# Attention on one Trainium2 core: the Wo projection and its add to x inside the attention loop

## What is computed

```
x = x + 0.5 * ffn0(layernorm(x))
x = x + attn0(layernorm(x), Wq, Wk, Wv, Wo, lam)
x = x + 0.5 * ffn0(layernorm(x))
x = x + 0.5 * ffn1(layernorm(x))
x = x + attn1(layernorm(x), ...)              # a gated delta rule
x = x + 0.5 * ffn1(layernorm(x))

attn0: q, k, v = x @ Wq, x @ Wk, x @ Wv; q, k = rope(q), rope(k)
  a1 = softmax(q[:64] @ k[:64] / 8), a2 = softmax(q[64:] @ k[64:] / 8)   # each row sees the last 64 keys
  diff = relu(a1 - lam[h] * a2); diff = diff / (sum(diff) + 1e-6)
  return concat_heads(diff @ v) @ Wo           # (1024, 2048) @ (2048, 256)
```

## Time and profile before

| | |
|---|---|
| three runs | 1872.32 us median (1869.02 to 1873.83) |
| profiled execution | 1875.38 us, its span 1873.4 us |
| PE, matmuls | 1599.8 us busy (85% of the span) |
| PE, weight loads | 1067.9 us (57%) |
| DVE | 1332.4 us (71%) |
| ACT | 1071.6 us (57%) |
| POOL | 41.2 us (2%) |
| attention loop | about 141 to 406.5 us from the span's start |
| projection with Wo, and add | 406.6 to 468.1 us |

### The profile page before, as it was taken

One profiled execution on the slowest core, in us unless ns is written; L12 is line 12 of the kernel. 1 busy time (PEld: TensorE's weight loads), 2 busy tenths in 40 slices (PEclk: granted clock), 3 DMA queues, 4 the chain that ended last, 5 costly groups with the idle time before them and its releaser, 6 DMA issues. The chain is left out here.

```text
span 1873.4 us, 32717 instructions
## 1 busy us (share of the span) xinstructions
PE 1599.8 (85%) x10728; PEld 1067.9 (57%) x10728; DVE 1332.4 (71%) x3702; ACT 1071.6 (57%) x2752; POOL 41.2 (2%) x49
## 2 busy tenths in 40 slices
PE   7867777689879857999999999999998999988678
PEld 3534434354344424676677767766766777677434
DVE  6648999830761347888988899889889888984121
ACT  6217888850621164577668766766676686653210
POOL 0000000000000000000000000000000000000000
PEclk9887998859899877999999999999999999989589
DMA  2022001000110020110211011011101110110010
GB/s 99 24 73 41 13 10 49 1 1 0 74 53 21 17 81 13 38 54 11 56 55 53 11 58 52 18 52 52 57 11 56 55 54 11 47 29 7 1 50 23
DMA packets 83989, 69.39 MB, mean 37 GB/s; under 512 B 58592, under 2 KB 72544, under 8 KB 82544
## 3 DMA queue, kind: packets, MB, share of 16 engines
q1 hardware_dynamic: 83824, 67.30, 12.0%
HBM read 58.32 MB, written 6.98 MB: 35 GB/s over the span
## 5 line engine op out<-in xcount | busy, mean ns | idle before, releaser
L1488 DVE SCALAR_TENSOR_TENSOR arena<-arena 128x1024 f32<-128x1024 f32 x144 | 184.2, 1279 | 33.6 <-ACT arena L1075 32.8
L762 PE MATMUL bank<-xt,arena 128*128 128x512 f32 x384 | 199.6, 654 | 4.5 <-ACT arena L1067 3.1
L602 PE MATMUL bank<-xt,arena 128*128 128x512 f32 (+2 forms) x384 | 178.8, 623 | 20.3 <-DMA arena<-f_ds 13.8
L1546 DVE COPY_PREDICATED arena<-arena,bank 128x512 f32<-128x512 int32 x160 | 185.6, 1179 | 0.0
L815 PE MATMUL bank<-arena 128*64 128x64 f32 x3072 | 144.1, 238 | 35.9 <-DVE arena L1568 21.9
L815 PEld LDWEIGHTS bank<-arena 128*64 128x64 f32 x3072 | 117.3, 144 | 84.0 <-issue 55.3
L1566 DVE TENSOR_TENSOR arena<-arena 128x512 f32<-128x512 f32 x224 | 157.0, 701 | 4.1 <-PE bank L815 3.7
L602 PEld LDWEIGHTS bank<-xt,arena 128*128 128x128 f32 (+2 forms) x384 | 70.9, 189 | 121.6 <-issue 99.2
L1008 ACT ACTIVATE arena<-arena 128x128 f32<-128x128 f32 x256 | 99.6, 390 | 33.5 <-DVE arena L1421 33.5
L762 PEld LDWEIGHTS bank<-xt,arena 128*128 128x128 f32 x384 | 74.3, 211 | 76.0 <-issue 73.0
L621 PE MATMUL bank<-arena 128*128 128x256 f32 (+2 forms) x384 | 101.7, 413 | 10.4 <-DVE arena L1313 9.6
(11 more groups left out here) (171 smaller groups left out, 3555.3 us busy)
## 6 DMA issues: line engine op xcount, KB each, us to landing
arena<-zero_scratch SPq DMA_DIRECT2D x29, 512.0 KB, 4.2
arena<-d_w SPq DMA_DIRECT2D x16, 519.0 KB, 6.5
arena<-beta_scratch SPq DMA_DIRECT2D x16, 512.0 KB, 5.5
arena<-f_up SPq DMA_DIRECT2D x2, 1408.0 KB, 6.7
arena<-w_scratch SPq DMA_DIRECT2D x2, 1376.0 KB, 6.1
arena<-f_idx SPq DMA_DIRECT2D x2, 1072.0 KB, 10.1
w_scratch<-arena SPq DMA_DIRECT2D x2, 1072.0 KB, 4.1
arena<-a_wq SPq DMA_DIRECT2D x16, 128.0 KB, 2.3
```

The source lines that it names most:

```text
L602: last = pe.matmul(bank[2 * w + n % 2][0:rows, :], (WU if f < 2 else WU1R)[:, w, k, m * P:m * P + rows], XT[:, k, hf * HALF:(hf + 1) * HAL ...
L762: last = pe.matmul(bank[b][:], DW[:, par, c:c + P], XT[:, k, rhs], start=(k == 0), stop=(k == KC - 1))
L1488: dve.scalar_tensor_tensor(out=CT[:, x], in0=RAW[:, x, 3 - j:3 - j + S], scalar=DW[:, par, tap:tap + 1], in1=CT[:, x], op0=ALU.mult, op1=A ...
L1546: dve.copy_predicated(out, mask, bank[b][:].rearrange("p (c b s) -> p c b s", c=8, s=s)).then_inc(free[b], 1)
```

## The change

The projection moves into the loop. For each group g and tile t, two halves of two heads each (`weighted`, 4 matmuls of 256 columns for both halves) have OT as the stationary operand and Wo as the moving one, so the result comes out untransposed in bank 5, two tiles beside each other. `out_parts` gives four slots to a pair of tiles: both halves of the first tile, a half of the second, the other half, nothing. So group 0 is projected in iterations 16 to 31, group 1 in 32 to 47, group 2 in 48 to 62, and group 3 in 63 to 70, one whole tile in each. DVE adds two tiles at a time to x in the iteration after their last half, ahead of `diff2`: 16 adds instead of 4. `weigh` shares bank 4 with `turn` now. Everything after `mask` comes one iteration later, and ACT's order is changed. Wo is loaded before the 12 loads of Wq. The transposes, YTR and its copies go.

```diff
+def out_parts(p):
+    if p < PAIRS - 1:
+        g, at = divmod(p - 2 * NT, 2 * NT)
+        j, step = divmod(at, 4)
+        return [(g, 2 * j + t, half) for t, half in (((0, 0), (0, 1)), ((1, 0),), ((1, 1),), ())[step]] if g >= 0 else []
+    return [(G - 1, p - PAIRS + 1, half) for half in range(2)] if p < PAIRS - 1 + NT else []
+
+def out_sums(p):
+    return [(g, t // 2) for g, t, half in out_parts(p - 1) if t % 2 and half]
...
+                sp.dma_start(WO, a_wo).then_inc(wo_loaded, 16)
                 for h in range(4, H):
                     sp.wait_ge(rp_done, ROPE_DONE["q", h - 4])
                     sp.dma_start(WQ[:, h % 4], a_wq[h]).then_inc(at_wq[h % 4], 16)
-                sp.dma_start(WO, a_wo).then_inc(wo_loaded, 16)
...
                     wait(pe, pt_copied, p)
+                    wait(pe, ot_copied, p - 1)
...
-                    o = bank[5][:, 0:2 * P].rearrange("p (i q) -> p i q", i=2)
+                    o = bank[4][:, 2 * P:4 * P].rearrange("p (i q) -> p i q", i=2)
...
+                def weighted(g, t, half):
+                    if half == 0:
+                        pe.wait_ge(wo_loaded, 16)
+                        pe.wait_ge(ot_copied, 16 * g + NT + t + 1)
+                        wait(pe, wo_added, 4 * g + t // 2)
+                    for h in range(2 * half, 2 * half + 2):
+                        last = pe.matmul(bank[5][:, t % 2 * D:(t % 2 + 1) * D], OT[:, 4 * g + h, t * P:(t + 1) * P],
+                                         WO[:, 4 * g + h, :], start=(h == 0), stop=(h == 3))
+                    if t % 2 and half:
+                        last.then_inc(wo_done, 1)
...
-                for p in range(PAIRS + 4):
-                    staggered(p, [(0, scores), (3, turn), (4, weigh)])
+                for p in range(PAIRS + NT):
+                    staggered(p, [(0, scores), (4, turn), (5, weigh)])
                     for m in rope_starts(p):
                         rope_project(m)
+                    for g, t, half in out_parts(p):
+                        weighted(g, t, half)
-            def project_out(a, u, ots):
...
-                project_out(0, 1, (ot_copied, PAIRS))
...
-                    wait(act, pv_done, p - 1)
+                    wait(act, pv_done, p)
...
-                             bank[5][:, 0:2 * P].rearrange("p (i q) -> p i q", i=2)).then_inc(ot_copied, 1)
-                for p in range(PAIRS + 5):
-                    staggered(p, [(3, pt_copy), (0, lambda p: exps(p, 0)), (2, norm), (0, lambda p: exps(p, 1)), (1, relu),
-                                  (4, ot_copy)])
-            def wo_copy(a):
...
+                             bank[4][:, 2 * P:4 * P].rearrange("p (i q) -> p i q", i=2)).then_inc(ot_copied, 1)
+                for p in range(PAIRS + 6):
+                    staggered(p, [(1, lambda p: exps(p, 0)), (4, pt_copy), (5, ot_copy), (3, norm), (1, lambda p: exps(p, 1)),
+                                  (2, relu)])
...
+                def add_out(g, j):
+                    dve.wait_ge(wo_done, 4 * g + j + 1)
+                    wait(dve, wo_added, 4 * (g - 1) + j + 1)
+                    x = X[:, 2 * j:2 * j + 2, :]
+                    last = dve.tensor_tensor(x, bank[5][:].rearrange("p (t d) -> p t d", t=2), x, ALU.add)
+                    last.then_inc(wo_added, 1)
+                    if g == G - 1:
+                        dve.wait_ge(wo_added, 4 * g + j + 1)
+                        dve.memset(TICK[:, 4 + j:5 + j], 0.0).then_inc(x_ready, 1)
...
-                for p in range(PAIRS + 2):
+                for p in range(PAIRS + NT + 1):
                     parts = rope_parts(p)
-                    staggered(p, [(2, norm1), (0, lambda p: mask(p, 0)), (2, norm2), (0, lambda p: mask(p, 1)), (1, diff1)])
+                    staggered(p, [(3, norm1), (0, lambda p: mask(p, 0)), (3, norm2), (0, lambda p: mask(p, 1)), (2, diff1)])
                     for m, part in parts[:len(parts) // 2]:
                         rope(m, part)
-                    staggered(p, [(1, diff2), (1, diff3)])
+                    for g, j in out_sums(p):
+                        add_out(g, j)
+                    staggered(p, [(2, diff2), (2, diff3)])
```

More of the change, by code:

```diff
@@ L280, in macaron @@
         A = Arena(arena, H * D)
-        YTR = arena[:, A.at:A.at + 2 * KC * HALF].rearrange("p (b n s) -> p b n s", b=2, n=KC)
         KZ = A.take(G, WIN + S)
@@ L380, in macaron @@
         ot_copied = sem("ot_copied")
-        wo_loaded, wo_done, wo_copied, wo_turned = sem("wo_loaded"), sem("wo_done"), sem("wo_copied"), sem("wo_turned")
+        wo_loaded, wo_done, wo_added = sem("wo_loaded"), sem("wo_done"), sem("wo_added")
         dr_const, dr_set = sem("dr_const"), sem("dr_set")
@@ L1036, in ot_copy @@
                     act.copy(OT[:, 2 * k:2 * k + 2, t * P:(t + 1) * P],
-                             bank[5][:, 0:2 * P].rearrange("p (i q) -> p i q", i=2)).then_inc(ot_copied, 1)
-                for p in range(PAIRS + 5):
-                    staggered(p, [(3, pt_copy), (0, lambda p: exps(p, 0)), (2, norm), (0, lambda p: exps(p, 1)), (1, relu),
-                                  (4, ot_copy)])
-            def wo_copy(a):
-                for n in range(4):
-                    act.wait_ge(wo_done, 4 * a + n + 1)
-                    act.copy(YTR[:, n // 2, n % 2, :], bank[n % 2][:]).then_inc(wo_copied, 1)
+                             bank[4][:, 2 * P:4 * P].rearrange("p (i q) -> p i q", i=2)).then_inc(ot_copied, 1)
+                for p in range(PAIRS + 6):
+                    staggered(p, [(1, lambda p: exps(p, 0)), (4, pt_copy), (5, ot_copy), (3, norm), (1, lambda p: exps(p, 1)),
+                                  (2, relu)])
             def dr_prelude():
@@ L1222, in _ @@
                 attention()
-                wo_copy(0)
             if count > 2:
@@ L1685, in _ @@
                 attention()
-                add_out(0, 1)
             if count > 2:
```

## The result

The changed kernel takes 1824.24 us (median of 4 runs, 1821.74 to 1829.46) against 1871.88 (4 runs): ratio 0.9744, 95% interval 0.972 to 0.9768, so 47.6 us or 2.6% faster. The prediction was 1831, range 1820 to 1854. The profiled execution has a span of 1823.5 us against 1873.4. One of the five executions of a later experiment, e3_old_lags, took 5042 us where the others took 1832 to 1842; the ratio leaves it out, the median counts it.

What follows compares the result with a forecast made beforehand. DVE was taken to bound the loop with rope, ACT without it, then PE alone for 61.6 us; -61.6 + 6.9 - 2.4 + 2 + 12.1 + 2 = -41.0 us from 1872.3 gave 1831, range 1820 to 1854.

Steps and rivals of the forecast that it cites:

- What is removed, and the tail: Behind the loop: the 61.6 us of PE alone go; the new PE-paced tail adds 12.1, plus 2 for half clock.
- The +2 for a stretch at half clock: In the tail: a stretch or two of PE's work at half clock adds 2 us.
- The adds on DVE: Iterations 19 to 55: ten adds of 0.69 us where DVE bounds, +6.9 us; two later ones hidden.
- Late scores: DVE's waits before the mask: six, 4.8 us, come at PE's half clock; half of that is gained, -2.4.
- Late PE: Iterations with rope: PE's added matmuls delay the next scores and pt_copy, +2 us, bounds 0 and 5.5.
- the worst iteration: Every eighth iteration: PE has two halves and a projection, 5.3 us; five such, 1.1 us over each.
- 0 for it, and 0.1 x 8 at most later: ACT's 15.8 us of waits for the mask go, but gain 0 where ACT is not the bound, little later.
- Costs put at nothing for ACT: ACT's queue: pt_copy's new wait for weigh of the pair before, holding back ot_copy, norm and exps, costs 0.
- the 12 that were named as a sign of being wrong: Sign against the forecast: ACT's pt_copy waiting for PE more than 12 us in all.
- A half at 0.244 us per record: PE's added matmuls: 256-column records at 0.244 us, a half of 4 records 0.98 us, all 62.5.
- the cold tail: Rival: PE at half clock from iteration 56 through the tail, +21.6 us, 1853 us; chance 0.12.
- PE as the bound: Rival: PE's waits for ACT stay, iterations take 4.55 us, not 4.2, 1847 us in all; chance 0.16.

Runs made afterwards that it cites:

- e3_old_lags: The changed kernel with the lags of before (turn 3, weigh 4, exps 0, norm 2, relu 1), ACT's changed order kept: 1838.4 us, 0.9805 of the kernel before.
- e8: The changed kernel with the free slot first, group 3 from iteration 64 and in banks 6, 7, 5, 6: 1824.1 us, 0.9744 of the kernel before.
- e4: The changed kernel without the 12 adds to x of the first three groups, a small memset in their place: 1809.0 us, 0.9662 of the kernel before.
- e2: The changed kernel's lags, ACT order, shared bank 4 and early Wo load, but the old dense projection behind the loop: 1861.0 us, 0.9927 of the kernel before.
- e10: The changed kernel with the free slot first and group 3 in banks 6, 7, 5, 6 from iteration 63: 1808.7 us, 0.9657 of the kernel before.

## Why the prediction was right

The direction held, and so did the main mechanism: the stretch with PE alone is gone, and the loop takes the projection for little. That the time within the loop came out as forecast is luck in part: errors of opposite sign, as large as what they left.

- **What is removed, and the tail**: -61.6 + 12.1 + 2 = -47.5 predicted; from the mask of pair 63 to the layer norm 72.3 became 24.8, -47.5. Two errors cancel in this match. The step had no wait on bank 5: PE waited 5.1 us for adds there, and e8 shows that without it the stretch is 5.8 shorter. And PE's work behind the mask, 23.1 us, was sized 4.1 too long, since e8 takes 19.0 at full clock: PE's iteration 63 begins 3.0 us before that mask (388.57 against 391.59), and a tile takes 1.82 us, not 1.96. The +2 for a stretch at half clock was real: eight records took 3.56 us instead of 1.89.
- **The adds on DVE**: +6.9 predicted, about 9.0 measured (e4). The mis-sized term is what the add delays, not the add: in iterations 31 and 47 it stood ahead of a rope sum for which PE's scores wait.
- **Late scores, -2.4 with ends at 0 and -4.8**: mis-sized, and split in two. The six waits away from a new group are all gone; their iterations take 23.0 us and took 28.9. The step gave more work on PE, and the clock with it, as the reason. The clock is full in these iterations now, but the waits are gone in e2 as well, without that work. But at a new group the scores became later: all masks together waited 9.5 us from 200 to 420 us, where they had waited 7.6.
- **Late PE, +2**: 2.0 by e4 against e2, and up to 2.4 more where iteration 16 is long. I had named the worst iteration and spread it over five places; it fell on two or three.
- **"0 for it, and 0.1 x 8 at most later", the stage**: the step that failed. Light iterations, in which ACT's chain was the bound, became shorter: 2.0 us in 16 to 55 (2.7, if iteration 53 is counted with its like, 49 and 51) and 1.7 in 56 to 62 (e2), and iterations 1 to 15 took 4 us less. All of e2 comes to 9.9 us in the profile and 13 in the medians. Of its 7.2 us in iterations 16 to 55 the late scores are the larger part, not the 15.8 us of waits for the mask.
- **The sum of iterations 16 to 55**: +6.5 predicted; the experiments give -7.2 (e2) + 2.0 (halves) + 9.0 (adds) + 1.4 (iteration 16) = +5.2, the profile +5.8. The forecast of the median missed 6.6 us, the profile 8.9: 5.0 lie in iterations 0 to 15, and 4.6 before the first mask, which is chance. So the last add ended at 416.3 us, not near 427.
- **Costs put at nothing for ACT**: pt_copy waits 21.7 us for weigh, more than the 12 that were named as a sign of being wrong. It cost little away from a new group: but for iteration 32, e4, which has the halves, is within 0.5 us of e2 in every iteration of 16 to 55. DVE is busy 91%, not over 93.
- **A half at 0.244 us per record**: halving a record of 512 columns, as the Trainium skill, "TensorE: Matmul & The Clock Gate", section "Back-to-back issue gap", would have it (columns / 2.4 GHz + 2.5 ns), gave 0.215. The trace agrees with the rule: within a run of such records they start 0.216 us apart. The row of 0.244 held some gaps of 0.31 us. In the loop a half takes 0.95 us until the next matmul begins (206.15 to 207.10), so for the sum the row's 0.98 was near, and the rule's 0.86 leaves out the change to other work.
- **The rivals**: the cold tail did not come; the clock was 0.87 in iterations 56 to 62 and 0.93 behind. The lower clock came only for a time, mostly after PE had waited at a new group. PE as the bound did not come either: its waits for ACT fell from 46.0 us (200 to 420 us) to 13.7. Those of weigh for ot_copy, 35.5, went; those of turn for norm rose from 10.5. Nothing behind the last add grew beyond chance.

## What to carry to other kernels

An engine that is not the bound on average can still hold up the loop where the load alternates. Compare iterations of the same kind with each other, and light ones with the engine's own work (3.55 us here against 3.24), not busy shares over the stretch: six long iterations at a low clock cost 5.7 us here and were gone with the new lags and order. When work is spread into a loop, look at the few iterations where a dependency lets the other engines run dry (here a new group's first scores), and keep both the new matmuls behind it and the new add ahead of it away. One bank for a spread accumulation needs a free slot before its next use; more banks, where they are idle, took PE's waits for the add away altogether (e8).

## What the runs showed of the hardware

After PE had idled 4.13 us at a new group, 16 small records took 1.13 us, not 0.67, and a projection 3.45, not 1.9, although PE was busy 85% of iterations 16 to 55. The 256-column work kept the clock up in iterations 56 to 62: 0.87 with the halves, 0.57 without them and otherwise the same pipeline (e2), 0.50 before. With halves and projections together it was 0.94 in iterations 16 to 55. At full clock, float32 records of 256 columns start 0.216 us apart: 24 of them took 5.35 us at the end of e8 and e10.
